# A routed ViT block on one core: paired expert scatters, expert bias inside the blocks, and the last low parts of the weights made by VectorE during the first blocks

## The reference

```python
h = patches @ W + b;  h = concat(cls_tok, h)
h = h + attention(layernorm(h))                  # causal, 12 heads of 16, output projection
x = layernorm(h)
gates = softmax(x @ Wg + bg);  top 2 of 8 -> combine (592 x 8, two gates in each row)
y[e] = gelu(x @ W1[e] + b1[e]) @ W2[e] + b2[e]   # 192 -> 768 -> 192
h = h + sum over e of combine[:, e] * y[e]
```

## Time and profile before

| what | value |
|---|---|
| time, median of 3 (lowest, highest) | 230.97 us (228.99, 231.61) |
| profiled execution: its own time, its span | 231.12 us, 229.3 us |
| TensorE busy, share of the span | 182.2 us, 79% |
| VectorE, ScalarE, GpSimd busy | 123.6, 99.9, 92.7 us |
| mean granted TensorE clock | 0.819 of full speed |
| chain that ended last | TensorE 56%, VectorE 17%, DMA 11% |

### The profile page before, as it was taken

How to read it: one execution, slowest core, us unless ns; L and a number is a source line. 1 busy time by engine, 2 the same in 40 slices (tenths; PEclk the granted TensorE clock), 3 DMA queues, 4 the chain that set the end, 5 groups by cost and what they waited for, 6 DMA issues and landing times.

```text
span 229.3 us, 3604 instructions
## 1 busy us (share of the span) xinstructions
PE 182.2 (79%) x993; PEld 142.5 (62%) x993; DVE 123.6 (54%) x388; ACT 99.9 (44%) x301; POOL 92.7 (40%) x71
## 2 busy tenths in 40 slices
PE   3999999979996999399692341758999999999710
PEld 2877444347683958159351230747999999999700
DVE  0124654826649374952749889953456456555300
ACT  2011221498894566272111337014656656656300
POOL 0012243489256019659265579100223423432340
PEclk9999999999979559555555555578999999999985
DMA  6956999999999401001039931120142233232111
GB/s 163 309 151 147 285 303 324 323 288 244 200 205 199 137 3 41 0 9 35 3 73 297 241 92 32 33 77 23 26 76 46 42 69 56 43 44 35 20 20 17
DMA packets 25655, 27.11 MB, mean 118 GB/s; under 512 B 4880, under 2 KB 21928, under 8 KB 25634
## 3 DMA queue, kind: packets, MB, share of 16 engines
q1 hardware_dynamic: 21378, 24.16, 41.0%
q0 software_dynamic: 4256, 2.69, 8.0%
HBM read 23.73 MB, written 8.64 MB: 141 GB/s over the span
## 4 chain that ended last, share of the span: by engine, by line
PE 56%; DVE 17%; DMA 11%; issue 5%; ACT 5%; SPq 2%; POOL 1%; ACTq 0%; POOLq 0%; DVEq 0%
PE bank L698 9%; DMA out_y<-y,tokblk 8%; PE bank L459 7%; PE bank L560 6%; PE bank L722 5%; PE bank L528 4%; PE bank L485 3%; PE bank L708 3%; PE bank L543 3%; DVE tablei L1209 3%; DVE pay L1112 2%; ACT probs L813 2%; PE bank L724 2%; PE bank L490 2%; DVE pay L999 2%
## 5 line engine op out<-in xcount | busy, mean ns | idle before, releaser
L442 POOL DMA_INDIRECT out_y<-y,tokblk x14 | 21.9, 1562 | 57.8 <-DMA out_y<-y,tokblk 25.3
L722 PE MATMUL bank<-we,hthi 128*128 x84 | 25.9, 370 | 1.4 <-DVE htlo L1241 1.4
L372 POOL TENSOR_TENSOR rstd<-veps,nhalf 111x1 f32<-111x1 f32 (+1 forms) x12 | 7.0, 583 | 47.6 <-DVE veps L983 47.6
L698 PE MATMUL bank<-we,xahi 128*128 x56 | 21.0, 374 | 1.4 <-DVE xb L1223 1.4
L405 POOL DMA_INDIRECT dispatched<-pay,rowu x12 | 16.5, 1374 | 12.1 <-DVE rowu L1138 10.3
L380 POOL TENSOR_TENSOR we<-raw,we 128x1152 fp32r<-128x1152 f32 x8 | 20.9, 2622 | 0.6 <-ACT we L869 0.6
L813 ACT ACTIVATE probs<-bank,sneg 111x111 f32<-111x111 f32 (+1 forms) x72 | 18.2, 355 | 6.7 <-DVE sneg L1067 6.7
L724 PE MATMUL bank<-we,htlo 128*128 x84 | 21.0, 251 | 0.0
L459 PE MATMUL bank<-wtok_sb,x_sb 128*111 128x192 f32 (+1 forms) x72 | 17.4, 402 | 4.0 <-DMA wtok_sb<-in_w_tok 4.0
L560 PEld LDWEIGHTS bank<-vp,pt 111*111 111x111 f32 (+1 forms) x144 | 17.5, 210 | 4.2 <-issue 4.2
L560 PE MATMUL bank<-vp,pt 111*111 111x17 f32 (+1 forms) x144 | 17.9, 269 | 2.2 <-issue 2.1
(11 more groups left out here) (152 smaller groups left out, 420.6 us busy)
## 6 DMA issues: line engine op xcount, KB each, us to landing
dispatched<-in_pad_rows SPq DMA_DIRECT2D x1, 5350.5 KB, 35.7
raw<-in_w SPq DMA_DIRECT2D x8, 576.0 KB, 11.7
raw<-in_w_a SPq DMA_DIRECT2D x8, 384.0 KB, 9.8
raw<-in_w_bb SPq DMA_DIRECT2D x8, 384.0 KB, 8.5
xin<-dispatched SPq DMA_DIRECT2D x14, 130.5 KB, 2.2
x_sb<-in_patches SPq DMA_DIRECT2D x5, 333.0 KB, 5.3
raw<-in_w_b SPq DMA_DIRECT2D x8, 192.0 KB, 8.4
wtok_sb<-in_w_tok SPq DMA_DIRECT2D x3, 192.0 KB, 3.3
```

Of the source, the lines that this page charges most:

```text
L442: pool.indirect_dma_start(out, bass.IndirectOffsetOnAxis(ap=tokblk[:, b:b + 1], axis=0), y[:, b % 2, :], None, compute_op=ALU.add).then_in ...
L698: last = mm(bank[1 + hf][:, 0:FH], x[:, :], w, start=(i == 0), stop=(i == 4))
L722: mm(o[:, 0:2 * D], hthi[:, f, :], w, start=(f == 0), stop=False)
```

## The change

1. Scatters paired: the outputs of block b and b-1 may be in flight together if both blocks belong to the same expert; if not, GpSimd waits for b-1 first. Each parity of b has a semaphore (`added[0]`, `added[1]`), and the value to wait for is read from a table (`T_TURN`). The rows of padding go to two sets of spare output rows, whose first fill is moved from SyncE to GpSimd's queue at the start.
2. Bias in blocks: all the per-tile bias steps go. b2 is split into parts once, and `layer2` gets a last matmul `taken` x `b2hl_sb` (16 rows); `taken` is made by one more VectorE instruction in `block_gates`. h is written after `h2_ready`.
3. Low parts: `split(e)` on VectorE makes all three low parts of expert e. Experts 5, 6 and 7 are done after `output(0)`, `output(1)` and `output(2)`. `layer1(b)` reads a wait value from the table (`T_LAST`) and waits for its own expert only.
4. Tail: the order on TensorE, ScalarE and VectorE is changed; ScalarE rounds experts 6 and 7 only after the last `gate_exp`; `xin` of blocks 0 and 1 is loaded before SyncE reads the number of blocks.

```diff
 pool:
-            split_w2(EARLY - 1)
             root(TILES - 1, 1)
             dispatch(TILES - 3); dispatch(TILES - 2); dispatch(TILES - 1)
-            for e in range(EARLY, E):
-                split_w2(e)
...
                     if b >= 1:
+                        turn = pool.value_load(tablei[0:1, T_TURN + b:T_TURN + b + 1], ...)
                     pool.wait_ge(y_ready, b + 1)
                     pool.wait_ge(gate_ready, b + 1)
+                    if b >= 1:
+                        pool.wait_ge(added[(b - 1) % 2], turn)
                     pool.indirect_dma_start(out, ..., y[:, b % 2, :], None, compute_op=ALU.add)
-                                                                  .then_inc(added, 16)
-                    pool.wait_ge(added, 16 * (b + 1))
+                                                                  .then_inc(added[b % 2], 16)
 pe, tail:
             out_project(TILES - 1)
+            ranks(TILES - 3)
             gates_t(TILES - 2)
             logits(TILES - 2)
-            gates_back(TILES - 3)
-            ranks(TILES - 3)
             gates_t(TILES - 1)
+            logits(TILES - 1)
             ranks(TILES - 2)
-            logits(TILES - 1)
-            gates_back(TILES - 2)
             ranks(TILES - 1)
 pe, blocks:
                 pe.wait_ge(xlo_ready, b + 1)
+                pe.wait_ge(lo_dve, pe.value_load(tablei[0:1, T_LAST + b:T_LAST + b + 1], ...))
...
-                    last = mm(o[:, 0:D], htlo[:, f, :], w, start=False, stop=(f == FC - 1))
-                last.then_inc(l2_done, 1)
+                    mm(o[:, 0:D], htlo[:, f, :], w, start=False, stop=False)
+                pe.wait_ge(gate_ready, b + 1)
+                mm(o[:, 0:D], taken[:, b % 3, :], b2hl_sb[:, :], start=False, stop=True).then_inc(l2_done, 1)
 vector, tail:
                     second_stats(TILES - 2)
-                    norm_apply(TILES - 2, 1)
                 if i >= LAG:
                     choose(i - LAG)
+            norm_apply(TILES - 2, 1)
             residual(TILES - 1)
...
-            for e in range(EARLY - 1, E):
-                split_w1(e)
 vector, blocks:
+                v.tensor_scalar(taken[:, b % 3, :], expertids_sb[:, 2:2 + BLK], table[0:2 * E, b:b + 1], None,
+                                ALU.is_equal)
...
                     output(b)
+                    if b <= E - EARLY:
+                        split(EARLY - 1 + b)
```

More of the change, by code:

```diff
@@ L287, in vit_block @@
         y_ready = sem("y_ready")
-        added = sem("added")
+        added = [sem(f"added{b}") for b in range(2)]
+        turns_ready = sem("turns_ready")
         fixed = sem("fixed")
@@ L406, in dispatch @@
                                             pay[0:n, t % 3, :], None).then_inc(scattered[t % 3], 16)
+            for s in range(2):
+                pool.dma_start(out[N + s * BLK:N + s * BLK + BLK, :], pad_rows[:, s, 0:D]).then_inc(added[s], 16)
             pool.wait_ge(fixed, 1)
@@ L672, in _ @@
             last.then_inc(count_done, 1)
-            gates_back(TILES - 1)
-            for t in range(TILES - 3, TILES):
-                bias2(t)
             pe.wait_ge(table_ready, 1)
@@ L1018, in _ @@
                     norm_apply(t - 1, 0)
+            dve.wait_ge(ld_rest, REST_LOADS)
+            step(v.tensor_copy(b2hi_sb[:, :], b2_sb[:, :]))
+            v.scalar_tensor_tensor(out=b2hl_sb[:, :], in0=b2hi_sb[:, :].bitcast(F32), scalar=expertids_sb[:, 0:1],
+                                   in1=b2_sb[:, :], op0=ALU.mult, op1=ALU.add).then_inc(b2_split, 1)
             dve.wait_ge(b1_raw, 16)
```

166 lines of the change are left out of this document (77 added, 89 removed).

## The result

After 20 runs of each kernel the changed one takes 232.14 us in the median (229.54 to 236.86), the one before 230.86 (226.69 to 235.67). The ratio is 1.011, with a 95% interval of 1.006 to 1.016: about 1% slower, where 2% faster was forecast. So the profiled execution of before is a typical one and that of after is a lucky one, 2.5 us under its median.

What follows compares the result with a forecast made beforehand. No single engine was the bound overall; TensorE set the block period. Shifts of -11.1 at layer1(0), +7.5 low parts, +1.4 bias and -2.1 scatters summed to -4.3 us, giving 226.6 us, range 221.8 to 230.6.

Steps and rivals of the forecast that it cites:

- Loop, -2.0: Loop up to the tail's start: gates_back, comb and the bias2 wait go, so the tail starts 2.0 us sooner.
- Tail, -8.9 from its start to the table: Tail: stalls of 3.1 and 6.0 us behind GpSimd's splits go; table ready at 133.6, a shift of -10.9 in all.
- Table to block 0, "the warm-up takes over as the wait that ends last": Before block 0: xin lands at 138.8 to 139.8, warm-up ends at 139.5; block_t(0) starts at 139.6, a shift of -11.8.
- The first block, +0.7: Before layer1(0): its wait-value read lies open once, 0.6 us, taking the shift from -11.8 to -11.1.
- Rival (a): Splits cost less, or the clock stays up in layer1(0) (1.7 us): sum -7 to -9, 222 to 224 us; chance 20%.
- Low parts, +7.5: Blocks 1 to 3: VectorE's 3.0 us splits leave TensorE idle 2.5 us in each, +7.5 us.
- Bias matmul, "0.1 per block": layer2 in each block: one matmul of 192 columns costs 0.1 us, +1.4 us over 14 blocks.
- In later blocks I cost that read at nothing: layer1 after block 0: wait-value read covered by the sequencer's 1.5 us lead; uncovered, up to 0.6 us in 13 blocks.
- Rival (c): The read in layer1 shows in the blocks, 0.6 us x 13 = 7.8: 234.4 us; chance 8%.
- Scatters, -2.1: End of the blocks: pairing works off the backlog; last scatter 0.9 us after output(13) instead of 3.03, -2.1 us.
- rival (d): Scatter pairing does nothing, +2.1, 228.7 us; also the case of the loop moving only -0.5; chance 12%.

Runs made afterwards that it cites:

- b_dve: Kernel before, with only the three split_w2 of experts 5 to 7 moved from GpSimd to VectorE after the table: 223.57 us, ratio 0.985.
- best3: best2 with SyncE's h writes behind xin of blocks 0 and 1, and their row numbers read before the wait for the scatters: 216.82 us, ratio 0.954.
- warm: Changed kernel with 36 instead of 18 warm-up matmuls and 12 more behind block_t(0): 231.92 us.
- early: Changed kernel with the three VectorE splits moved ahead of block 0, right after the table's instructions: 225.68 us.
- pad128: Changed kernel with the bias matmul's operands padded by zeros from 16 to 128 rows: 233.73 us.
- pad_en: Changed kernel with bias operands on 128 rows, splits before block 0 and no wait-value read in layer1: 224.36 us, ratio 0.973.
- best: Changed kernel with bias operands on 128 rows, splits before block 0 and 36 + 12 warm-up matmuls: 221.36 us, ratio 0.975.
- best2: best without the wait-value read in layer1: 219.29 us, ratio 0.954.
- nobias: Changed kernel without the bias matmul and the taken instruction, so the output lacks b2: 229.4 us, ratio 1.005.
- early_noread: early without the wait-value read in layer1, TensorE waiting once for all splits before block 0: 224.6 us.

## Why the prediction was wrong, step by step

- *Loop, -2.0*: in the profiled pair -4.2, in the five further traces -3.0 to +0.6. The stall of the cast remained (5.11 us). The size is within what the start varies by, and no run took this term alone: it is not settled. Of the -4.2 in the profiled pair 1.9 us is the quick second patch tile, which this term has no part in.
- *Tail, -8.9 from its start to the table*: right in kind, low in size: 26.3 us became 14.0, -12.3. Counted from its start, `rows(4)` was done at 8.5 us (9.6 in my layout), `rows(5)` at 11.0 (13.6) and the table at 14.0 (17.3): I had left 0.4 to 0.9 us of waiting for dispatches in each `choose`, and the trace shows one wait of 0.5. `b_dve` shows the cause.
- *Table to block 0, "the warm-up takes over as the wait that ends last"*: failed. It ended 3.9 us too early, because the landing of the last dispatch is the wait that ends last. I had the last dispatch issued 1.8 us before the table, and it was issued 0.3 before; and I took 3.9 us for its landing from the rows of another kind of scatter, and it took 5.5. These two make 3.1 us, and the stretch took 9.2 us where I had 6.0 (9.2 to 10.1 over the six traces). I also had SyncE "past the tiles of h"; it issued those writes until 131.3, but that was still before the landing and cost nothing here. The cold read of 1.12 us lay within my bounds; `best3` shows that 1.4 us behind the landing can be saved.
- *The first block, +0.7* (the 0.6 of the read, with 0.1 lost in rounding): the open read of `layer1(0)` held (0.65), but it takes 1.9 us more than before in the further traces, since `layer1(1)`'s read is open too (0.63) and the bias matmul takes its 0.46. Rival (a)'s "the clock stays up in `layer1(0)`" needed a warm-up that lasts until xin is there; `warm` shows that it is worth about 2 us. With the surplus of loop and tail these cancel by luck in the profiled pair (`output(0)` at -10.9, forecast -11.1), but not in the further traces: there `output(0)` moves by -6.5 to -10.5.
- *Low parts, +7.5*: held: 6.5 measured over the period now, 2.5 to 2.7 a block over that of before. Since `early` runs at the median 6.5 us faster, the step also prices the choice of place. (Expert 5 is first used in block 7, seven blocks after its split and not four; the wait is free either way.)
- *Bias matmul, "0.1 per block"*: this is the step that failed most. Its row was of 128-row matmuls; a 16-row one costs 0.44 (4.78 against 4.34), and 13 blocks of 0.43 give 5.6 where 1.4 stood: +4.2 us. On 128 rows it costs the 0.1 that I had (0.11).
- *"In later blocks I cost that read at nothing"*: failed too, hidden by the former. It costs 0.11 to 0.14 a block once the matmul is on 128 rows (`pad128` against `pad_en`, `best` against `best2`), and 0.23 over before where there is no bias matmul (`nobias`). The lead of 1.5 us on the sequencer did not last with a second read in each block. Rival (c) had the mechanism, with a price of 0.6. In after itself it costs nothing beyond block 1, since the 16-row matmul hides it (`early` and `early_noread` have the same period).
- *Scatters, -2.1*: -2.8 in the profile, right in size and wrong in reason. Most of it comes without the pairing, from the longer period and the shorter landings, since a serial chain at 4.78 ends with a lag of 0.69 and at 4.46 of 0.58. The pairing is worth 0.4 us in the trace at 4.78 and 0.15 to 0.25 at 4.46; rival (d), that it does nothing, was nearer in that.

Sum in the profiled pair: -10.9 at `output(0)`, +12.2 in the blocks, -2.8 for the scatter and -0.2 behind it make -1.6 (unrounded -10.86, +12.22, -2.76). Forecast was -4.3; the blocks carry +3.3 of the difference, the scatters -0.7. The five further traces have `output(0)` 0.3 to 4.4 us later than the profiled one, which turns a small gain into the measured small loss. So the step that failed is the bias matmul, put at 0.1 us a block and measured at 0.44, and next to it the wait that ends last ahead of block 0, which the surplus of loop and tail hides in the profiled pair. What sets the early or late start stayed open: two places where it arises are named above, and no experiment took them apart. Nor do I know what made the two groups of `pad128`.

## What to carry to other kernels

In this kernel a small matmul among large ones was not priced by its columns: ask how many rows its neighbours use, and if they use more, try filling its rows with zeros. Work taken from one engine's hidden time must land in hidden time of the other: the same nine instructions cost 6.5 us between blocks and 0 to 0.4 beside the wait for the first block's data, until that wait was shortened in `best3` and they cost 1.4. And when a long wait shortens, list all that had been hidden behind it (another queue's issues, a landing, a first read, a warm-up timed for the old gap), since two costs that overlap show only one at a time, and the second appears when the first is mended.

## What was not expected of the hardware

- The 16-row matmul between 128-row ones: 0.46 us more between the weight loads around it, 0.33 of it gone when its rows were filled to 128 (0.31 us from the last load of `layer2` to that of `hidden_t`, with one load more than the 0.18 of before).
- Software-issued DMAs beside VectorE's two-input instructions: 2.02 to 2.09 us for an issue instead of 1.55. The forecast had set the rule of the Trainium skill ("SBUF — State Buffer", section "SBUF: two separate sides") aside by the row at 136.72; the first three scatters of after bear it out for GpSimd's side, though none waits until the splits have ended (the first is issued by 155.05, the third split ends at 155.67), while VectorE's splits kept their 0.94 and 1.34 us. It costs nothing here, as the scatter is not late.
- The issue of a DMA of h on SyncE's queue took up to 3.65 us right behind the issues of the large weight loads (12.17 for six), 0.66 in the mean (3.95 for six) 15 us later in `best3`.
- Two register reads per block on TensorE's sequencer: a period of 4.57 us with no bias matmul at all, where one read alone allowed 4.34, and 0.19 to 0.29 us of idle time ahead of `layer1` with nothing waited for.
